# Two of the four DMAs that carry the row maxima are issued by ScalarE, behind its copy of the maxima

## The reference

```python
x = x + attn(layernorm(x))            # 16 heads of 8, rope on q and k, causal, softmax over 128 keys
x = x + cross(layernorm(x), ctx)      # 16 heads of 8, softmax over 77 context rows
x = x + ffn(layernorm(x))             # router over 8, one of 7 experts per token, plus a shared expert

def softmax_part(q, k, v):            # both attentions
    scores = einsum('bhqd,bhkd->bhqk', q, k)
    probs = exp(scores - max(scores, axis=-1)) / sum(...)
    return einsum('bhqk,bhkd->bhqd', probs, v)
```

## Time and profile before

| what | us |
|---|---|
| three timed runs | 1310.55, 1306.17, 1289.0 |
| their median | 1306.17 |
| the profiled execution's own time | 1296.01 |
| its span, from first to last instruction | 1294.2 |
| busy in the span: PE | 1181.2 (91%) |
| DVE | 856.7 (66%) |
| ACT | 745.1 (58%) |
| POOL | 630.9 (49%) |

### The profile page before, as it was taken

One profiled execution on the slowest core, in us unless ns is written; L12 is line 12 of the kernel. 1 busy time (PEld: TensorE's weight loads), 2 busy tenths in 40 slices (PEclk: granted clock), 3 DMA queues, 4 the chain that ended last, 5 costly groups with the idle time before them and its releaser, 6 DMA issues.

```text
span 1294.2 us, 47343 instructions
## 1 busy us (share of the span) xinstructions
PE 1181.2 (91%) x14512; PEld 842.9 (65%) x14513; DVE 856.7 (66%) x2780; ACT 745.1 (58%) x1555; POOL 630.9 (49%) x1488
## 2 busy tenths in 40 slices
PE   1799999999999999999999999999998949999996
PEld 1356766666767667776677666677667736666664
DVE  3445777777777777777777777777775435555553
ACT  0445666666666666676666666667665214444442
POOL 1334565555556555565556655556553203333333
PEclk9657999899999999999999999999999559999998
DMA  7200000000000000000000000000000021222120
GB/s 181 85 8 10 26 28 27 23 22 21 21 23 27 22 21 21 25 25 22 21 21 25 25 22 21 21 24 26 25 19 17 21 72 55 62 61 61 58 66 9
DMA packets 66667, 44.37 MB, mean 34 GB/s; under 512 B 24135, under 2 KB 61579, under 8 KB 66592
## 3 DMA queue, kind: packets, MB, share of 16 engines
q1 hardware_dynamic: 55856, 30.63, 8.7%
q0 software_dynamic: 5312, 12.18, 2.7%
q10 hardware_dynamic: 5424, 0.59, 0.5%
HBM read 23.85 MB, written 18.29 MB: 33 GB/s over the span
## 4 chain that ended last, share of the span: by engine, by line
PE 72%; DMA 10%; SPq 10%; issue 2%; ACT 2%; ACTq 1%; DVE 1%; POOL 0%; DVEq 0%; POOLq 0%
PE pv L1106 10%; SPq L383 10%; DMA arena<-arena 9%; PE scores L1046 7%; PE scores L1148 6%; PE scores L1155 5%; PE scores L1254 5%; PE ro L1271 5%; PE scores L1255 5%; PE pj L1129 4%; PE scores L1070 3%; PE scores L1058 3%; PE ro L1123 3%; PE ro L1174 2%; PE ro L1115 2%
## 5 line engine op out<-in xcount | busy, mean ns | idle before, releaser
L972 ACT ACTIVATE arena<-scores 128x1024 f32<-128x1024 f32 (+1 forms) x256 | 261.5, 1021 | 131.2 <-PE scores L1070 113.4
L661 DVE TENSOR_REDUCE arena<-scores 128x8 f16<-128x1024 f32 (+1 forms) x256 | 254.1, 993 | 41.5 <-PE scores L1081 39.8
L894 ACT ACTIVATE arena<-st 128x128 f16<-128x128 f16 (+2 forms) x256 | 154.6, 604 | 114.4 <-PE st L1189 68.3
L1046 PE MATMUL scores<-causal 64*128 64x256 bf16 x1024 | 106.1, 288 | 47.8 <-DMA arena<-arena 47.7
L1106 PE MATMUL pv<-arena 128*32 128x128 f32 (+1 forms) x4096 | 146.3, 286 | 0.0
L432 POOL TENSOR_TENSOR arena<-arena,eps 128x1 f32<-128x1 f32 x192 | 35.9, 187 | 204.2 <-DVE arena L643 204.2
L441 POOL TENSOR_TENSOR arena<-arena,neg_half 128x1 f32<-128x1 f32 x192 | 106.5, 555 | 29.0 <-POOL arena L432 10.9
L1106 PEld LDWEIGHTS pv<-arena 128*32 128x32 f32 (+1 forms) x4096 | 109.3, 114 | 13.1 <-issue 0.9
L1046 PEld LDWEIGHTS scores<-causal 64*128 64x128 bf16 x1024 | 29.6, 95 | 130.7 <-DMA arena<-arena 76.6
L854 DVE SCALAR_TENSOR_TENSOR half_hid<-tanh_s,scores 128x512 f32<-128x512 f32 x70 | 48.1, 688 | 90.7 <-ACT tanh_s L1011 90.7
L894 ACT ACTIVATE arena<-arena 128x512 f16<-128x512 f32 (+2 forms) x192 | 91.8, 478 | 12.2 <-POOL arena L460 10.6
(11 more groups left out here) (168 smaller groups left out, 2747.7 us busy)
## 6 DMA issues: line engine op xcount, KB each, us to landing
x_tile<-xs SPq DMA_DIRECT2D x70, 129.0 KB, 2.0
arena<-arena SPq DMA_DIRECT2D x512, 4.0 KB
arena<-in_x_dram SPq DMA_DIRECT2D x64, 64.0 KB
out_dram<-pay SPq DMA_DIRECT2D x64, 64.0 KB, 1.6
arena<-in_ctx_dram SPq DMA_DIRECT2D x64, 38.5 KB
w_gate<-in_L_ffn_gate_w_dram SPq DMA_DIRECT2D x7, 256.0 KB, 4.6
w_up<-in_L_ffn_up_w_dram SPq DMA_DIRECT2D x7, 256.0 KB, 4.9
w_down<-in_L_ffn_down_w_dram SPq DMA_DIRECT2D x7, 256.0 KB, 5.3
```

The source lines that it names most:

```text
L661: v.tensor_reduce(nmax[:, n, :].rearrange("p (m r s) -> p r m s", r=2, s=SLOT)[:, u, :, 0:HG], pair(s)[:, :, 0:HG * keys].rearrange("p m ( ...
L894: return a.activation(to, of, ACT.Copy)
L972: a.activation(e32[0:rows, 2 * n + u, :], scores[0:rows, 1024 * s:1024 * (s + 1)], ACT.Exp).then_inc(sexp_done[n][u], 1)
L1046: t.matmul(pair(s)[:, m].rearrange("p (g h k) -> p h g k", h=2, k=P // 2)[:, h], causal[rows, turn_of, P * h:P * (h + 1)], causal[rows, tu ...
```

## The change

SyncE issues the DMAs of the partition groups j = 0 and 1 as before, and ScalarE those of j = 2 and 3, right behind its own copy of the maxima. ScalarE first waits for the semaphore of its own copy. The transfers, their sizes, the semaphore `max_rows` and its counts stay as they are. Both attentions are changed, so ScalarE issues four DMAs for each batch and SyncE four in place of eight.

```diff
@@ rows_of_max, SyncE @@
                 wait(sync, nmT_ready[n], b + 1)
-                for j in range(4):
+                for j in range(2):
                     sync.dma_start((qkT, qkT2)[n][SLOT * j + 3 * HD:SLOT * j + 3 * HD + HG, p, 0:HG * P].rearrange("p (g q) -> p g q", g=HG),
                                    nmaxT[SLOT * j:SLOT * j + HG, n, p, :].unsqueeze(1).to_broadcast([HG, HG, P])
                                    ).then_inc(max_rows[n][p], 16)
@@ nmT_copy, ScalarE @@
                 copy(nmaxT[:, n, p, :], st16[:, 0:P]).then_inc(nmT_ready[n], 1)
+                wait(act, nmT_ready[n], b + 1)
+                for j in range(2, 4):
+                    act.dma_start((qkT, qkT2)[n][SLOT * j + 3 * HD:SLOT * j + 3 * HD + HG, p, 0:HG * P].rearrange("p (g q) -> p g q", g=HG),
+                                  nmaxT[SLOT * j:SLOT * j + HG, n, p, :].unsqueeze(1).to_broadcast([HG, HG, P])
+                                  ).then_inc(max_rows[n][p], 16)
```

## The result

The changed kernel takes 1347.15 us (median of its runs), the kernel before 1307.0 us with the runs taken beside it. The ratio is 1.035, with a 95% interval of 1.022 to 1.048: slower. The profiled execution took 1345.2 us, 49.2 us more than the one before. The time lies inside the stated range (1295 to 1355), but the forecast of 1323 us was too low and its "within 2%" was wrong.

The account below looks back on a forecast made before the run. TensorE, busy 91%, was taken to bound the kernel. 58 stops of 1.04 us less 40.7 us of waits won back give +19.6 us; with 3 us off for the clock, 1306.17 becomes 1323 us, range 1295 to 1355.

Parts of the forecast that it names:

- DMA side: Before the self_for_exp masks: TensorE's wait for the self-attention maxima disappears, gaining 40.7 us in all.
- The price of an issue: On ScalarE's queue: 0.68 us per DMA issue, 1.36 us for two, with ends of 0.42 and 0.83 us.
- The n = 1 issues at nothing: ScalarE's cross-attention issues cost 0, since tanh's 0.47 us wait for PE just covers the delay.
- The stop before ctxT_of: ScalarE's n = 0 issues delay xT_copy 0, so TensorE stands still 1.04 us before ctxT_of in each step.
- The step: One batch of the loop: about 15.05 us in place of 14.67.
- The clock: TensorE's falls to the lower clock level become rarer, as shared_down's large products follow the stop; worth some 3 us.
- The sum of +19.6 us: Over the loop: 58 stops of 1.04 us before ctxT_of, less 40.7 us of waits won back before the masks.
- rival 3: TensorE's clock falls more often after the longer stop: 15 falls adding 22 to 38 us, about 1353 us; 9%.
- Rival 1: SyncE's and ScalarE's issues exclude each other: full exclusion 1404 us, 7%; milder, 0.83 us per issue, 1343 us, 11%.
- Rival 2: ScalarE is not held by its issues, so ctxT_of runs on time: 1265 us, 6%; intermediate form 1295 us, 8%.
- The base: The sum was set upon the kernel before's median of three runs, 1306.17 us; its profiled execution took 1296.01.
- the forecast itself: Whole kernel: 1323 us, 1.3% more, called "within 2%" on the slow side; 59%.

Follow-up runs that it names:

- e11: Kernel before, with SyncE issuing two self-attention (n = 0) DMAs and nobody the other two, those maxima left out: 1243.4 us, ratio 0.954.
- e1: Changed kernel with only the cross-attention (n = 1) DMAs split with ScalarE, n = 0 all on SyncE: 1309.3 us, ratio 0.999.
- e2: Changed kernel with only the self-attention (n = 0) DMAs split with ScalarE, n = 1 all on SyncE: 1356.3 us, ratio 1.041.
- e3: Changed kernel with ScalarE issuing one n = 0 DMA, behind xT_copy 0, and n = 1 all on SyncE: 1256.8 us, ratio 0.967.
- e6: Changed kernel with ScalarE issuing one n = 0 DMA, ahead of xT_copy 0, and n = 1 all on SyncE: 1273.7 us, ratio 0.978.
- e4: Changed kernel with the transposes of stacks made three times, right ahead of ctxT_of, filling the stop: 1304.3 us, ratio 1.001.
- e9: Changed kernel with the transposes of stacks made twice, half filling the stop before ctxT_of: 1304.3 us, ratio 1.009.
- e10: Changed kernel with the transposes of stacks2 made three times, 4 us away from the stop: 1381.4 us, ratio 1.054.
- e7: Kernel before, with project_kv2's one matmul made twice right ahead of the masks, filling its stop: 1285.3 us, ratio 0.984.
- e5: Changed kernel with ScalarE issuing two n = 0 DMAs, behind xT_copy 0, and n = 1 all on SyncE: 1265.7 us, ratio 0.971.
- e8: e3 with the transposes of stacks made three times in the first eight batches only: 1242.2 us, ratio 0.954.

## Why the prediction was right or wrong

- **DMA side: right.** The wait before the masks is gone in the changed kernel, and e11 gives the step at 13.94 us, where the prediction had 14.0.
- **The price of an issue: right.** 1.32 us for two on ScalarE, where 1.36 was taken; the ends of 0.42 and 0.83 us were not needed.
- **The n = 1 issues at nothing: right,** shown by e1.
- **The stop before ctxT_of: right in place, slightly short in size.** The place is shown by e1, e2, e3 and e6, which move or halve the issues. PE comes to ctxT_of 605.69 - 603.21 = 2.48 us after the transpose of the maxima, against 609.39 - 608.01 = 1.38 before (starts of the same two groups in PE's timeline), so 1.10 us later and not 1.04. The two issues ended at 605.18 and the next copy began at 605.36: the hand-over is 0.18 us, where 0.05 was set.
- **The step: 15.05 predicted, 15.08 and 15.24 measured.** In every second step, the one in which shared_down begins a new turn of the loop, shared_down starts 0.49 us after the start of the group ahead of it (605.91 to 606.40), and 0.35 us in the others. e2, e4, e6, e9 and e10 have this alternation as well, e1 and the kernel before have not. Its cause is open: a branch at the loop's turn that shows because PE has just stood still would be a guess, and e4, whose stop is filled, has it too. The sum of +19.6 us is mis-sized: the longer step costs 29.5. Of the 10 us between, the stop of 1.10 us gives about 3.5, the alternation about 5, and about 3 come from taking off 0.70 us, the average wait, where the ordinary step had waited 0.65.
- **The clock: wrong, and this is the step that failed.** The prediction said that "such falls" would "become rarer rather than more frequent, worth some 3 us", since the stop is now followed by shared_down's large products. They went from four steps in 59 to twelve, and cost about 21 us more than before. e2 has them with the stop alone, e4 takes them away by filling the stop while the length of the step stays, and e10 keeps them, if shorter ones, with the same kind of work placed elsewhere. So the stop of 0.94 us is their cause; its neighbours did not protect it. What in the chip sets the length of a fall no run shows. I had argued from what follows the stop. The 1.5 us stop ahead of the 5 us at 0.50 was a row on what a longer stop does, and I gave it 9%, in rival 3. That rival named the right mechanism, with 15 falls where there were twelve, and its 22 to 38 us hold the 24 us by which the clock went over its term in the sum.
- **Rival 1, issuers that exclude each other: refuted.** SyncE and ScalarE issued together from 603.86. ScalarE's issue took 649 ns in the median and SyncE's 672, up from 638. SyncE's pair, begun at 603.86, took 1.45 us and not the 2.7 of full exclusion. The Trainium skill ("Perfetto Trace Analysis", section "DMA Instruction — HWDGE (DVE, Sync)") describes an exclusive lock. Here it would have to be held for a small part of an issue only, or not be shared by these two engines; no run tells which.
- **Rival 2, ScalarE not held: refuted** by the row of the copy at 605.36.
- **The base, and the luck in the total.** Between the two traces the time grew by 49 us where the sum had 17: the step is 10 us over its term and the clock 24 us (21 more in place of 3 less). Yet the median is only 24 us over the forecast, because I laid the sum upon the median of the kernel before, 1306.17, which is 10 us above its traced run. The range held because I had stretched it to rival 3; the forecast itself, with its 59%, did not come true. The base also holds low clock that a change can win back or lose: e7 has the same step of 14.66 us and takes 1285 us, and e11, e5 and e6, without the old stop, have no fall between 120 us and their last ctxT_of. The sum had no term for the start and 3 us for the loop.

## What to carry to other kernels

In this kernel moving a DMA issue to another engine moved its 0.65 us in front of everything behind it there; look up who reads the very next result, and put the issue behind the one that is due first. One place further down turned a loss of 4.1% (two issues, e2) into a gain of 2.9% (the same two, e5) or 3.3% (one, e3). When a change leaves TensorE standing in every step, price the clock as well as the stop: here the longer step cost 29.5 us and the falls of the clock about 21 more, and redundant matmuls in the stop gave the clock back. Price the falls from a trace of your own, since stops of 0.5 us at the same place cost none.

## What the runs showed of the hardware

- 1024 extra transposes of 128x128 in fp16 made the changed kernel 43 us faster (1347.2 to 1304.3 us), with the steps as long as they were and a higher granted clock. A second matmul for kv2 in each batch made the kernel before 1.6% faster, with the step unchanged too.
- A stop of 0.5 us in every step (e9) left the granted clock at 1.00 between 120 and 985 us; stops of 0.92 us on average at the same place went with 0.94 (e2), 0.96 (the changed kernel) and, with longer steps around them, 0.98 (e10).
- At the start of the pipeline (40 to 120 us) the granted clock was 0.92 with the filling and 0.77 without, and 0.89 in e8 against 0.75 in e3. It was 1.00 in e5 without any filling, so that the filling did it is not shown. e8 was 14.6 us faster than e3, of which the traces show 5.6 us ahead of the fifth ctxT_of.
- Two engines issuing small DMAs at once slow each other by little: 672 ns in place of 638 on SyncE. ScalarE began an issue 0.13 us before the end of the ACTIVATE ahead of it where nothing made it wait for that (e5: 605.20, where the ACTIVATE of 605.06 took 0.27 us).
